# Token and channel diffusion with routed experts, one core: late steps of the last body re-placed, and the first batch's second square and key loads given to ScalarE

## The reference

```
x = x + layernorm(attn(layernorm(x)))
  attn(x): x = x + token_diffusion(ln1(x)) * gamma1      # 16 heads of 16
           x = x + channel_diffusion(ln2(x)) * gamma2    # 8 heads of 32 channels
  token_diffusion: qk = x @ Wqk, v = x @ Wv
           logits = (2 qk.qk' - |qk|^2 - |qk'|^2) / 4 * tau;  softmax(logits) v @ Wo
x = x + layernorm(moe(layernorm(x)))
  moe: p = softmax(x @ w_router), the 2 best of 8 experts per token,
       sum of p_e * (gelu(x @ w1_e + b1_e) @ w2_e + b2_e)    # 256 -> 1024 -> 256
```

## Time and profile before

| | |
|---|---|
| timed runs | 1079.21 us median of 3 (1075.86 to 1083.97) |
| profiled execution | 1083.45 us, of which its span 1081.6 |
| busy share of the span | TensorE 90%, ScalarE 68%, VectorE 62%, GpSimd 37% |
| mean granted clock of TensorE | 0.964 |
| first scores start | 31.41 us |
| last body (b = 7) | from about 446 to 514 us |
| experts | from 516 us to the end |

### The profile page before, as it was taken

The page is one execution under the profiler, slowest core; times in us unless marked ns, Lnnn a source line. Parts: engine busy times, 40 slices in busy tenths (PEclk is TensorE's granted clock), DMA queues, the critical chain, the costliest instruction groups (busy, mean ns, idle before and its releaser), DMA issues.

```text
span 1081.6 us, 16809 instructions
## 1 busy us (share of the span) xinstructions
PE 978.8 (90%) x5468; PEld 661.8 (61%) x5468; DVE 675.0 (62%) x1882; ACT 730.4 (68%) x1124; POOL 403.6 (37%) x348
## 2 busy tenths in 40 slices
PE   5799999999999999978789998999999999998960
PEld 3223545454553555434488887888888888887850
DVE  5236185564838554553785588667766777677857
ACT  3788777777868777756636565677666676666836
POOL 4101020413222140304234356855555455454435
PEclk9899999999999999989899999999999999999985
DMA  7674716346181684813312443866655545567739
GB/s 274 139 235 82 266 38 228 108 127 224 52 272 40 239 290 145 317 47 101 144 60 103 104 113 70 243 183 152 154 159 138 171 123 123 121 181 212 214 52 290
DMA packets 57695, 171.12 MB, mean 158 GB/s; under 512 B 10384, under 2 KB 26896, under 8 KB 51728
## 3 DMA queue, kind: packets, MB, share of 16 engines
q1 hardware_dynamic: 38698, 137.99, 38.3%
q0 software_dynamic: 18768, 31.76, 15.3%
q10 hardware_dynamic: 150, 0.41, 0.2%
HBM read 98.55 MB, written 71.57 MB: 157 GB/s over the span
## 4 chain that ended last, share of the span: by engine, by line
PE 66%; DVE 12%; ACT 7%; issue 6%; DMA 4%; POOL 3%; another core or an unknown queue 2%; ACTq 0%; SPq 0%; DVEq 0%; POOLq 0%
PE PH L1760 15%; PE PO L979 7%; PE PS L996 7%; PE PB L1059 6%; PE PY L1791 5%; PE PB L1791 4%; PE PY L1796 3%; ACT E L603 3%; PE PA L1027 3%; PE PY L1792 2%; PE PA L1046 2%; PE PB L1792 2%; PE PT L1771 1%; DVE HP L1701 1%
## 5 line engine op out<-in xcount | busy, mean ns | idle before, releaser
L603 ACT ACTIVATE E<-PS,VV 128x1024 f32<-128x1024 f32 x256 | 271.6, 1119 | 76.0 <-PE PS L996 62.7
L1760 PE MATMUL PH<-XP,W1P 128*128 128x512 f32 (+1 forms) x1104 | 232.1, 368 | 13.3 <-DVE HP L1701 6.9
L1760 PEld LDWEIGHTS PH<-XP,W1P 128*128 128x128 f32 x1104 | 185.0, 192 | 55.0 <-DVE HP L1701 10.5
L1528 POOL DMA_INDIRECT choice_rows<-Y,DI x78 | 130.7, 1675 | 116.5 <-DVE Y L1661 93.7
L996 PE MATMUL PS<-OPB,OPA 102*128 102x512 bf16 x512 | 140.3, 388 | 13.4 <-ACT E L603 7.2
L1701 DVE TENSOR_TENSOR HP<-PH,HP 128x512 fp32r<-128x512 f32 x156 | 106.7, 686 | 65.2 <-ACT HP L1607 61.9
L979 PE MATMUL PO<-E,VA 128*32 128x512 f32 x1024 | 145.5, 619 | 0.0
L1602 ACT ACTIVATE PH<-PH,B 128x512 f32<-128x512 f32 (+1 forms) x184 | 107.5, 596 | 51.3 <-PE PH L1760 41.6
L996 PEld LDWEIGHTS PS<-OPB,OPA 102*128 102x128 bf16 x512 | 36.7, 98 | 160.5 <-ACT E L603 83.6
L1593 ACT CAST W2P<-WG 128x512 fp32r<-128x512 f32 x92 | 56.6, 621 | 105.2 <-PE PB L1792 63.4
L469 POOL DMA_INDIRECT expert_rows<-PAY,SLOT x64 | 63.0, 984 | 155.9 <-issue 81.9
(11 more groups left out here) (244 smaller groups left out, 1540.6 us busy)
## 6 DMA issues: line engine op xcount, KB each, us to landing
expert_rows<-ZERO SPq DMA_DIRECT2D x8, 4160.0 KB
WG<-experts SPq DMA_DIRECT2D x23, 1152.0 KB
WG<-experts SPq DMA_DIRECT2D x23, 1028.0 KB
OPB<-q_parts SPq DMA_DIRECT2D x192, 64.0 KB
q_parts<-QP SPq DMA_DIRECT2D x48, 128.0 KB
OPA<-q_parts SPq DMA_DIRECT2D x31, 192.0 KB
choice_rows<-ZERO SPq DMA_DIRECT2D x1, 5120.0 KB, 14.4
X<-x SPq DMA_DIRECT2D x8, 512.0 KB, 8.0
```

The lines of the kernel that those rows point to most:

```text
L603: a.activation(E[:, s % 2, h, :, :], PS[:, u % 2, :, :], ACT.Exp, scale=vec("tau_t")[:, 4 * (s // 2) + h:4 * (s // 2) + h + 1]).then_inc(e ...
L1528: g.indirect_dma_start(out=ys, out_offset=IND(ap=DI[:, t % 3, i:i + 1], axis=0), in_=Y[:, t % 2, i, :], in_offset=None, compute_op=ALU.add ...
L1760: last = m.matmul(PH[:, u % BANKS, at:at + w], W1P[:, a, k * HID + c * P:k * HID + c * P + P], XP[:, o, k, 0:w], start=(k == 0 and (a, o) ...
```

## The change

`LAST_AT` is re-placed: `z3t0` from position 4 to 6, `z3t1` from 5 to 6, `logits` from 6 to 7, `soft` and `top` from 7 to 8; `prefix` stays at 9, `begin` goes from 9 to 10. For batch 0 alone, ScalarE squares the second half of qk itself, from PSUM, between its two copies, having waited for GpSimd's square of the first half (the semaphore counts both); GpSimd leaves its second square out. And ScalarE issues the keys' loads of group 0 behind its first copy of the values, not the second.

```diff
-LAST_AT = {0: ['chan'], 1: ['chan_add'], 2: ['chan_stats'], 3: ['chan_norm'], 4: ['z3t0'], 5: ['z3t1'], 6: ['logits'], 7: ['soft', 'top'],
-           9: ['prefix', 'begin']}
+LAST_AT = {0: ['chan'], 1: ['chan_add'], 2: ['chan_stats'], 3: ['chan_norm'], 6: ['z3t0', 'z3t1'], 7: ['logits'], 8: ['soft', 'top'],
+           9: ['prefix'], 10: ['begin']}
@@ GpSimd, qk(m)
                 def step(b, par):
+                    if isinstance(b, int) and b == 0 and m == 1:
+                        return
                     pool.wait_ge(qf_ready, KC * b + m + 1)
                     g.tensor_tensor(SQ[:, m, :], QF[:, m, :], QF[:, m, :], ALU.mult).then_inc(sq_ready, 1)
@@ ScalarE, qk(m)
                     a.copy(QF[:, m, :], bank(b, 2 + m)).then_inc(qf_ready, 1)
+                    if isinstance(b, int) and b == 0 and m == 1:
+                        act.wait_ge(sq_ready, 1)
+                        a.activation(SQ[:, m, :], bank(b, 2 + m), ACT.Square).then_inc(sq_ready, 1)
                     a.copy(QP[:, m, 0, :], bank(b, 2 + m)).then_inc(pre_free, 1)
@@ ScalarE, vv(i)
-                    if isinstance(b, int) and b == 0 and i == 1:
+                    if isinstance(b, int) and b == 0 and i == 0:
                         act.wait_ge(q_stored[0], PARTS)
                         load_keys(act, b, 0)
```

## The result

The change takes 5.5 us off the median: 1073.84 us (12 runs) against 1079.31 (12 runs). The ratio, formed over the runs and not from the two medians, is 0.9938, 95% interval 0.9920 to 0.9956, which makes 6.7 us. Three more measurements of the same code, each beside runs of the kernel before on the same chip, gave 0.9914 (0.9890 to 0.9939), 0.9950 (0.9918 to 0.9981) and 0.9945 (0.9923 to 0.9967). The mean of the four is 0.9937, 6.8 us. Forecast were 9.8 us and 1069.4, range 1064.5 to 1076.5: direction and range hold, the gain is smaller than reckoned, and it is within 1%. By the time alone, 1073.84 lies nearer to the two lesser rivals (1071.5 to 1073, and 1074) than to the forecast, so only the profiles can say which terms came.

The account below looks back on a forecast made before the run. TensorE, busy 90% of the span, was taken as the bound, gains coming where it idles. Last body -6.8, gathers -1.0 and start -2.0 make -9.8 us: profiled 1083.45 to 1073.7, median 1069.4, range 1064.5 to 1076.5.

Parts of the forecast that it names:

- the two lesser rivals (1071.5 to 1073, and 1074): Start gives nothing, 0 to +1.3 us (chance 0.15); last body's wait only moves, its gain falling to about 3 (0.10).
- The removed wait (part 1): Last body: 7.9 us wait for batch 5's normalised rows goes, new waits take 3 back; `prefix` 6.8 us earlier.
- no low clock from 462 on: Sign in the changed kernel's profile: TensorE's clock not low in the last body from 462 us on.
- the longer wait at `unit0`: Experts' start: TensorE's wait for gathered rows grows from 2.1 to about 3 us; low clock behind it not counted.
- `begin` (part 2): Last body, position 9 to 10: TensorE's 2.2 us wait for `DG` goes, but nothing counted, as gathered rows decide.
- carried over: GpSimd's chain from the slots to the experts' first transposes keeps its 23 us, moving 6.8 us earlier.
- The gathers' term (-1.0): Before the experts: second weights' load runs further ahead of the fourth gather; 1.0 us gained, bounds 2 gained, 1 lost.
- The start (part 3): First batch: keys load 1.5 to 2 us earlier, first scores at 29.1 to 29.5; -2.0 us, bounds 0 and -2.8.
- the rival that all terms fall well (-11.9): Undisturbed gather, high clock at first scores, start -2.6, last body -7.3: -11.9 us, so 1067; chance 0.32.
- the slower one: TensorE stays at 1.2 GHz through the experts' first unit; 24 us of it make 1081 or more; chance 0.04.
- the lower bound of the last body: Least gain from parts 1 and 2 together: 5 us, where 7.8 was forecast, upper bound 9.5.

Follow-up runs that it names:

- the four profiles of the old order: Kernel before, plus three with its late steps unmoved: whole start change (ratio 0.9982), only the keys' loads moved (0.9985), only the square moved (0.9997).
- `after_again`: The changed kernel, unaltered, run again for an undisturbed profile: 1066.49 us against 1074.94 for the kernel before, ratio 0.9914.
- `hold_first`: The changed kernel, with the first expert's first weights' load held until the last body's eight scatters have landed: ratio 0.9929 to the kernel before.
- `after_third`: The changed kernel, unaltered, measured again beside later kernels: 1073.87 us against 1080.53 for the kernel before, ratio 0.9950.
- `after_fourth`: The changed kernel, unaltered, measured once more beside later kernels: 1074.75 us against 1082.37 for the kernel before, ratio 0.9945.
- `late_alone`: The kernel before with only the `LAST_AT` steps re-placed, start as before: 1068.0 us against 1074.94, ratio 0.9932.
- `square_alone`: The kernel before with only batch 0's second square moved from GpSimd to ScalarE, keys' loads as before: ratio 0.9997.
- the single-edit kernels: The kernel before with only the keys' loads moved (ratio 0.9985), and with only the square moved to ScalarE (0.9997).
- the first four experiments: The changed kernel again (1066.49 us), its late steps alone (1068.0), its start alone (1073.6), and it with `begin` at position 9 (ratio 0.9941).
- the last four: The changed kernel again (ratio 0.9945), with `begin` at 9 (0.9901), with first weights held (0.9929), with second weights held (0.9949).
- `hold_second`: The changed kernel, with the first expert's second weights' load held until the first four gathers have landed: ratio 0.9949 to the kernel before.

## Why the prediction was right, and where its sum was too large

- **The removed wait (part 1): right.** The waits that I placed one by one came out: 1.96 us at the bank for 1.85, L862 ready 1.06 us ahead of its transposes for 1.0, the change at `prefix` 6.8 us where the clock stays high, for 6.8. That it fits to a tenth is partly luck, as the four profiles of the old order differ by 1.1 us there (+43.15 to +44.25).
- **The term missed there is the clock.** I took the bank wait at its length. It costs 1.6 us more in five of eight profiles, as TensorE falls to 1.2 GHz behind it. With it `prefix` gains 5.2, over all eight 5.8, over the four whose experts are compared below 6.5. My sign "no low clock from 462 on" failed in those five. The Trainium skill ("TensorE: Matmul & The Clock Gate", HAM oscillation) has idle gaps of TensorE bring the half clock; I had set that against the longer wait at `unit0` alone. The traces agree at this shorter wait in five of eight: in `after_again` the low stretch runs from 469.0 to 472.4, right behind it.
- **`begin` (part 2): the zero was right, its reasons half.** TensorE's gain is hidden by the wait for gathered rows, as written. That GpSimd's chain is "carried over" was not: moving `begin` moves the first weights' load closer to the last scatters, and the first gather comes 1.5 us later (15.42 us behind the slots on the average of the four changed kernels of the next point, 13.92 in the four old orders). `hold_first` shows that this load is the cause. In these four profiles it is the largest term that the sum left out.
- **The gathers' term (-1.0) failed as a net.** From the fourth gather to the experts it is 5.63 us on the average of the four old orders and 4.57 in the four with the changed late steps (`after_again`, `after_third`, `after_fourth`, `late_alone`): 1.1 gained, as put. But that is no proof of the reason that I gave: the four old ones range from 4.36 to 6.59, the new from 3.34 to 5.98, and the second load, which I put 1.4 us ahead of the fourth gather's issue, was 4.1 and 3.8 us ahead in `after_again` and `late_alone` and 0.2 and 0.7 behind in `after_third` and `after_fourth`. The size is luck in part. The 1.5 of the point above take the term back. The experts start 69.74 us behind `chan` on the average of the four old orders, 63.72 on that of the same four changed ones: the last body gives 6.0 us, for 7.8 forecast: 6.5 at `prefix` for 6.8, 1.5 lost at the scatters, 1.1 gained at the gathers.
- **The start (part 3): right in mechanism, -1.5 for -2.0.** `Square` costs its copy's spacing, 0.48, and no table load. The Trainium skill ("ScalarE: Activation LUTs", Table sets) does not name square among the functions of every set; the one table load of `square_alone` decides that it needed no switch here. I had the earlier store as a mere balance to the 0.48 us; the single-edit kernels show that without `Square`'s move half of the gain is missing. What fell short is the landing of the queries' norms: they were issued up to 0.7 us later than the 27.05 that I kept (+11.53 from the copy), as this load waits for the norms' store, which is later and lands in 3.1 to 3.8 us behind the keys' loads for 1.7 before. And the first scores follow 2.4 to 3.0 us behind that issue, where I took 2.
- **The sum.** 6.0 and 1.5 make 7.5 from the profiles, where the four measurements have 6.8 on the mean. Measured by these, the gain came out a quarter to a third below the forecast; the rival that all terms fall well (-11.9) did not come. Nor did the slower one: in the hundred microseconds behind the experts' first transposes no low stretch lasted longer than the 6.8 us of before. And the lower bound of the last body, written as 5, should have been 4.5 by its own terms (5.5 and 1 lost), which changes nothing here.

## What to carry to other kernels

Re-placing a step behind its late input is worth the wait plus what the work behind it lost at the low clock, less the new waits. But count two steps that share a bank as one step with a copy between, and put another engine's work there: `z3t0` and `z3t1` one position apart had `prefix` 0.7 us earlier than both together at the same clock, in the one profile of it. Where a step that releases a large transfer moves, look at what the transfer now meets: here it met the scatters that the next phase waited for. And two loads that an engine waits for together are worth moving only as far as the later one moves; which edit lets it land earlier had to be found by doing each alone.

## What the runs showed that I had not expected

- Behind the same wait of TensorE of 1.96 us, the same instructions ran at 1.2 GHz in five executions of eight and at 2.4 GHz in three.
- From the experts' first transposes to the end of the span, code that no edit touches, the profiles take 556.2 to 568.8 us: 565.3 before, 556.2 to 557.0 in the first four experiments, 563.7 to 568.8 in the last four. The first four ran on one chip and the last four on another, where the kernel before took 1074.94 and 1082.37 us. That is more than the whole change moves, and is why seven microseconds need a median of many runs on the same chip; one profiled span says little. Part is the clock: between 520 us and the tail the granted clock falls twice in `after_again` and seven times in `hold_second`. What starts them was not tried.
- Between 488 and 508 us, other profiles of the changed kernel (`after_third`, `after_fourth`) have gaps of 1 to 2 us on ScalarE, for some of which the profile names nothing on this core that ended them, and TensorE finishes the last body 22.1 to 22.4 us behind the slots instead of 17.8. The wait for the gathered rows hid them. Their cause stays open.
